# A second buffer for x in a 33-step attention loop: x fetched and normalized one step further ahead, its fold split around the fold of the weights, and the even half of the output copied into the output buffer

## What is computed

```python
q = fft(layernorm(x))              # along the 512 positions, per channel; x is (8, 512, 2048)
corr = ifft(q * conj(fft(ctx)))    # real part
w, idx = top_k(corr, 12); w = softmax(w)
out = sum_i w_i * ctx[min(idx_i + pos, 511)]
x = x + out
x = x + ffn(layernorm(x))          # routed low-rank FFN: gate from top 16 of 64 experts, z = x A^T, out = z_gated B^T
```

## Time and profile before

| | us |
|---|---|
| median of 3 runs | 2494.78 (2491.77 to 2495.44) |
| profiled execution, whole | 2492.05 |
| its span | 2490.2 |
| first `ctx_cyclic` of step 2 to that of step 27 (25 steps) | 132.73 to 1323.34 |
| steps 27 to 30 (no statistics in them) | 1323.34 to 1502.80 |

### The profile page before, as it was taken

One profiled execution on the slowest core, in us unless ns is written; L12 is line 12 of the kernel. 1 busy time (PEld: TensorE's weight loads), 2 busy tenths in 40 slices (PEclk: granted clock), 3 DMA queues, 4 the chain that ended last, 5 costly groups with the idle time before them and its releaser, 6 DMA issues.

```text
span 2490.2 us, 29447 instructions
## 1 busy us (share of the span) xinstructions
PE 2305.9 (93%) x9728; PEld 1560.6 (63%) x9728; DVE 1772.1 (71%) x3937; ACT 946.5 (38%) x1744; POOL 1567.6 (63%) x1006
## 2 busy tenths in 40 slices
PE   3799999999999999999999998669999999999999
PEld 1455655655655555565555565448878878878877
DVE  2787888788888888788878878745555555656652
ACT  2354344344444434434434534323333333333330
POOL 4887887888787887888788885534334333334330
PEclk7899999999999999999999999789999999999999
DMA  5224223223222322322321312544444444444431
GB/s 192 93 77 139 72 73 131 85 72 123 94 72 96 120 72 85 131 73 72 135 82 55 103 62 101 191 144 162 152 161 161 150 160 164 150 160 166 151 129 51
DMA packets 111468, 290.13 MB, mean 117 GB/s; under 512 B 7168, under 2 KB 7296, under 8 KB 110208
## 3 DMA queue, kind: packets, MB, share of 16 engines
q1 hardware_dynamic: 111360, 288.81, 33.6%
HBM read 221.68 MB, written 67.11 MB: 116 GB/s over the span
## 4 chain that ended last, share of the span: by engine, by line
PE 46%; POOL 31%; DMA 10%; DVE 6%; ACT 5%; issue 2%; SPq 0%; POOLq 0%; DVEq 0%; ACTq 0%
DMA xf<-in_x_dram 8%; POOL r_f L1217 8%; PE z L492 5%; PE out L492 5%; PE evac L509 5%; PE out L494 5%; PE out L493 5%; PE z L494 5%; PE z L493 5%; PE pair L522 4%; ACT xf L1010 4%; POOL xf L1200 3%; POOL half_fold L1207 3%; POOL half_fold L1197 3%; POOL half_fold L1198 3%; POOL xf L1201 3%
## 5 line engine op out<-in xcount | busy, mean ns | idle before, releaser
L1252 POOL TENSOR_TENSOR rows<-rows,cin 128x1024 f32<-128x1024 f32 x48 | 116.8, 2434 | 398.0 <-DMA rows<-out_dram 291.2
L593 PE MATMUL pair<-r_f,back 128*128 128x512 f32 x768 | 334.9, 592 | 1.5 <-DVE prod L787 1.5
L1217 POOL TENSOR_TENSOR r_f<-prod 128x1024 f32<-128x1024 f32 x128 | 302.6, 2384 | 17.7 <-DVE prod L787 17.7
L593 PEld LDWEIGHTS pair<-r_f,back 128*128 128x128 f32 x768 | 145.8, 190 | 171.9 <-issue 168.4
L565 PE MATMUL lag<-lags,p_f 128*128 128x256 f32 x1024 | 234.3, 382 | 12.9 <-DVE e L808 12.9
L492 PE MATMUL pair<-w_hi,wts_hi 128*128 128x512 f32 x512 | 206.9, 404 | 33.1 <-DVE w_lo L881 23.7
L565 PEld LDWEIGHTS lag<-lags,p_f 128*128 128x128 f32 x1024 | 193.8, 192 | 40.2 <-issue 13.8
L492 PE MATMUL out<-b_hi,zt_hi 128*128 128x512 f32 x512 | 208.0, 406 | 1.5 <-ACT zt_hi L1163 1.5
L492 PE MATMUL z<-a_hi,xt 128*128 128x512 f32 x512 | 207.6, 406 | 0.0
L1178 ACT ACTIVATE xt<-tp 128x512 fp32r<-128x512 f32 x128 | 73.1, 597 | 338.0 <-PE tp L637 338.0
L494 PE MATMUL z<-a_hi,xt 128*128 128x512 f32 x512 | 201.4, 393 | 0.0
(11 more groups left out here) (143 smaller groups left out, 5494.7 us busy)
## 6 DMA issues: line engine op xcount, KB each, us to landing
vf<-in_ctx_dram SPq DMA_DIRECT2D x32, 1024.0 KB, 5.1
xf<-in_x_dram SPq DMA_DIRECT2D x32, 1024.0 KB, 8.2
out_dram<-att_sb SPq DMA_DIRECT2D x32, 1024.0 KB, 5.2
rows<-out_dram SPq DMA_DIRECT2D x64, 512.0 KB, 3.7
cin<-out_dram SPq DMA_DIRECT2D x64, 512.0 KB, 4.1
xin<-in_x_dram SPq DMA_DIRECT2D x64, 512.0 KB, 3.7
out_dram<-rows SPq DMA_DIRECT2D x64, 512.0 KB, 2.6
stat_in<-in_x_dram SPq DMA_DIRECT2D x28, 1024.0 KB, 7.5
```

Of the source, the lines that this page charges most:

```text
L593: return nc.tensor.matmul(pair_ps[:, bank, :], back[:, 3 * bank + n, :], r_f[:, row, :], start=n == 0, stop=n == 2)
L1217: nc.gpsimd.tensor_tensor(dst, prod[:, slot, 0:2, :], prod[:, slot, 2:4, :], ALU.add).then_inc(add_done, 1)
L1252: nc.gpsimd.tensor_tensor(half, first, second, op).then_inc(c_added, 1)
```

## The change

Group g of x now lives in `xfs[g % 2]` with a semaphore `x_loaded[g % 2]` for each. SP loads group i+2 in step i, as its first DMA of the step, when PE has read group i; group 1 is loaded before the loop. The load of `stat_in` moves to after `v_last` and is made one step earlier. ACT normalizes group i+2 in step i, after the copies of the correlation and after `root`. POOL's `fold_x` is cut in two: `begin_fold_x(i+1)` stands between `fold_w` of tiles 0, 1 and of tiles 2, 3, and `end_fold_x(i+1)` stands after the products of x. `invert` on DVE and `normalizers` on POOL move from after the fourth product of the weights to after the second. ACT copies the even half of the output into `att_sb[:, 2:4]` instead of `even_sb`, and now waits for the store of the step before; DVE works in place on it. `first_tiles` no longer waits for products before it fetches `cin` and `xin`.

```diff
-        xf, vf, half_fold, stat_in = sb("xf", [P, 4, CH]), sb("vf", [P, 4, CH]), sb("half_fold", [P, 4, CH]), sb("stat_in", [P, LT, CH])
+        xfs = [sb(f"xf{n}", [P, 4, CH]) for n in range(2)]
+        vf, half_fold, stat_in = sb("vf", [P, 4, CH]), sb("half_fold", [P, 4, CH]), sb("stat_in", [P, LT, CH])
...
-                sp.dma_start(xf[:], at_group(x_t, k, r, off)).then_inc(x_loaded, 16)
+                sp.dma_start(xfs[(3 + r + off) % 2][:], at_group(x_t, k, r, off)).then_inc(x_loaded[(3 + r + off) % 2], 16)
...
+            load_x(-1, 1, 1)
...
-                if s and not is_step(i, 0):
-                    next_stat()
-                if f:
-                    sp.wait_ge(pair_ready, pair_x(i, 1) + 1)
-                    load_x(k, r, 1)
+                if i + 2 < GROUPS:
+                    sp.wait_ge(pair_ready, pair_x(i, 1) + 1)
+                    load_x(k, r, 2)
...
                     load_last(k, r, 1)
+                if (i - 2) // GPB + 2 < B:
+                    sp.wait_ge(stat_used, LT * (i + 3))
+                    load_stat((i - 2) // GPB, (i - 2) % GPB, stat_in[:], stat_loaded)
...
-                sp.wait_ge(prod_ready, prod_w(i, 3) + 1)
-                sp.wait_ge(dc_put, i)
                 for h in range(2):
                     load_others(0, 0, h)
...
-                if s and r == 3:
-                    invert(k + 2)
+                        if n == 1 and s and r == 3:
+                            invert(k + 2)
...
-                    if not is_step(i, 1):
-                        dve.wait_ge(stored, 16 * (i - 1))
-                    nc.vector.tensor_tensor(att_sb[:, 0:2, :], even_sb[:], pair_ps[:, 2:4, :], ALU.add)
-                    nc.vector.tensor_tensor(att_sb[:, 2:4, :], even_sb[:], pair_ps[:, 2:4, :], ALU.subtract).then_inc(att_done, 1)
+                    nc.vector.tensor_tensor(att_sb[:, 0:2, :], att_sb[:, 2:4, :], pair_ps[:, 2:4, :], ALU.add)
+                    nc.vector.tensor_tensor(att_sb[:, 2:4, :], att_sb[:, 2:4, :], pair_ps[:, 2:4, :], ALU.subtract).then_inc(att_done, 1)
...
-                if f:
-                    norm_inputs(k, r, 1)
-                    norm(k, r, 1, range(LT))
-                if a:
+                    if is_step(i, 0):
+                        norm_inputs(k, r, 1)
+                        norm(k, r, 1, range(LT))
                     minus(v_neg[cur][:, 5, :], v_neg[cur][:, 3, :], 6 * i + 6)
...
                 if s and r == 3:
                     root(k + 2)
+                if i + 2 < GROUPS:
+                    norm_inputs(k, r, 2)
+                    norm(k, r, 2, range(LT))
...
-                        act.wait_ge(att_done, i - 1)
-                    nc.scalar.activation(even_sb[:], pair_ps[:, 0:2, :], ACT.Copy).then_inc(even_copied, 1)
+                        act.wait_ge(stored, 16 * (i - 1))
+                    nc.scalar.activation(att_sb[:, 2:4, :], pair_ps[:, 0:2, :], ACT.Copy).then_inc(even_copied, 1)
...
-                    for t in range(CT):
+                    for t in (0, 1):
+                        fold_w(i - 1, t)
+                if f and b:
+                    begin_fold_x(i + 1)
+                if b:
+                    for t in (2, 3):
                         fold_w(i - 1, t)
...
                 if f:
-                    fold_x(i + 1)
+                    end_fold_x(i + 1)
                     begin_fold_v(i + 1)
...
+                        if n == 1 and s and r == 3:
+                            pool.wait_ge(normed, LT * (i + 2))
+                            normalizers(k + 2)
```

More of the change, by code:

```diff
@@ L165, in build_program @@
         r_f, back = sb("r_f", [P, 8, CH]), sb("back", [P, 12, P])
-        even_sb, att_sb = sb("even_sb", [P, 2, CH]), sb("att_sb", [P, 4, CH])
+        att_sb = sb("att_sb", [P, 4, CH])
         ones, rstd, shift = sb("ones", [P, 2]), sb("rstd", [P, LT]), sb("shift", [P, LT])
@@ L198, in build_program @@
         consts_set = sem("consts_set")
-        x_loaded, v_loaded, last_loaded, normed = sem("x_loaded"), sem("v_loaded"), sem("last_loaded"), sem("normed")
+        x_loaded = [sem(f"x_loaded{n}") for n in range(2)]
+        v_loaded, last_loaded, normed = sem("v_loaded"), sem("last_loaded"), sem("normed")
         x_half, x_ready, v_half, v_ready = sem("x_half"), sem("x_ready"), sem("v_half"), sem("v_ready")
@@ L376, in _ @@
             sp.dma_start(back[:].rearrange("p n m -> p (n m)"), tables["back"]).then_inc(tables_loaded, 16)
+            load_x(-1, 1, 1)
             def body(k, r, a, b, f, s):
                 i = 4 * k + 3 + r
-                def next_stat():
-                    sp.wait_ge(stat_used, LT * (i + 2))
-                    load_stat(k, r, stat_in[:], stat_loaded)
-                if s and not is_step(i, 0):
-                    next_stat()
-                if f:
-                    sp.wait_ge(pair_ready, pair_x(i, 1) + 1)
-                    load_x(k, r, 1)
-                if s and is_step(i, 0):
-                    next_stat()
+                if i + 2 < GROUPS:
+                    sp.wait_ge(pair_ready, pair_x(i, 1) + 1)
+                    load_x(k, r, 2)
+                if is_step(i, 0):
+                    sp.wait_ge(stat_used, LT * 2)
+                    load_stat(k, r, stat_in[:], stat_loaded)
                 if f:
@@ L521, in x_spectrum @@
                     for part, (t, fold) in enumerate(((4, 0), (1, 3)) if n == 0 else ((2, 2), (3, 1))):
-                        last = nc.tensor.matmul(pair_ps[:, 2 * n + part, :], fwd[:, t, :], xf[:, fold, :], start=True, stop=True)
+                        last = nc.tensor.matmul(pair_ps[:, 2 * n + part, :], fwd[:, t, :], xfs[i % 2][:, fold, :], start=True, stop=True)
                     last.then_inc(pair_ready, 1)
@@ L1009, in norm @@
                     t = slice(j, j + 1)
-                    nc.scalar.activation(xf[:, j, :], xf[:, j, :], ACT.Identity, bias=shift[:, t], scale=rstd[:, t]).then_inc(normed, 1)
+                    part = xfs[(3 + r + off) % 2][:, j, :]
+                    nc.scalar.activation(part, part, ACT.Identity, bias=shift[:, t], scale=rstd[:, t]).then_inc(normed, 1)
             def norm_inputs(k, r, off):
-                act.wait_ge(x_loaded, 16 * (4 * k + 3 + r + off) + 16)
+                g = 4 * k + 3 + r + off
+                act.wait_ge(x_loaded[g % 2], 16 * (g // 2 + 1))
                 act.wait_ge(norm_ready, NORM_OPS * (k + quarter(r, off)[1]) + NORM_OPS)
@@ L1190, in _, with begin_fold_x, end_fold_x @@
         def _(pool):
-            def fold_x(g):
+            def begin_fold_x(g):
+                xf = xfs[g % 2]
                 pool.wait_ge(normed, LT * g + LT)
-                if is_step(g, 1):
+                if g == 1:
                     pool.wait_ge(x_ready, 1)
                 else:
-                    pool.wait_ge(v_ready, max(g, 1) if isinstance(g, int) else g)
+                    pool.wait_ge(v_ready, max(g, 1))
                 nc.gpsimd.tensor_tensor(half_fold[:, 0:2, :], xf[:, 0:4:2, :], xf[:, 1:4:2, :], ALU.add)
                 nc.gpsimd.tensor_tensor(half_fold[:, 2:4, :], xf[:, 0:4:2, :], xf[:, 1:4:2, :], ALU.subtract).then_inc(x_half, 1)
+            def end_fold_x(g):
+                xf = xfs[g % 2]
                 pool.wait_ge(x_half, g + 1)
@@ L1262, in _ @@
             normalizers(0)
-            fold_x(0)
+            begin_fold_x(0)
+            end_fold_x(0)
             def body(k, r, a, b, f, s):
@@ L1276, in body @@
                         add_products(prod_x(i, n), n, p_f[:, 2 * n:2 * n + 2, :])
+                if is_step(i, 0):
+                    begin_fold_x(1)
                 if f:
-                    fold_x(i + 1)
+                    end_fold_x(i + 1)
                     begin_fold_v(i + 1)
@@ L1285, in body @@
                         add_products(prod_w(i, n), n % 2, r_f[:, 2 * blk:2 * blk + 2, :])
+                        if n == 1 and s and r == 3:
+                            pool.wait_ge(normed, LT * (i + 2))
+                            normalizers(k + 2)
                 if is_step(i, GROUPS):
                     add_x(1, 0, 1)
-                if s and r == 3:
-                    pool.wait_ge(normed, LT * (i + 2))
-                    normalizers(k + 2)
                 if f:
```

## The result

The changed kernel takes 2410.31 us (median of 4 runs, 2406.42 to 2414.86) against 2495.11 (4 runs), a ratio of 0.9663, 95% interval 0.9640 to 0.9686: 3.4% faster. The forecast was 2405 with a range of 2393 to 2430. The profiled execution took 2407.21 us, its span 2405.4, where before it was 2490.2.

The account below looks back on a forecast made before the run. The loop through x's load, norm and POOL's vf held PE, itself nearly full and the next bound. Savings of 85.3 us (steps 2 to 26) and 3.1 (27 to 30) took 2492.05 to 2403.7; named 2405, range 2393 to 2430.

Parts of the forecast that it names:

- What bounds the kernel before: Loop of 47.62 us a step: x's DMA, ACT's norm, then POOL until vf, for which PE waits; PE nearly full.
- A step of PE: 44.1: PE's step when nobody is late: step 15's 47.02 us less three stalls, 2.9 together, leaves 44.1.
- rival B: DVE's row update and POOL block each other: update up to 2.4 us later, 14.6 in all, 2420; chance 0.14.
- Load and norm ahead: x's transfer (7.84 us) and ACT's norm (2.94) leave the loop; the 1.4 us wait on w_lo goes.
- The split fold: begin_fold_x fits POOL's idle place before weigh; POOL ends 2.2 us early where it was 1.2 late.
- DVE: Product 2 no longer waits 4.07 us for POOL; output sum 0.6 into the next step; stalls on evac_sin go.
- Root steps: Seven steps with root: PE's spectrum 2 waits for DVE, 0.4 us per step; the moved norm costs nothing.
- Even half, SP, ends: Even-half copy and store, SP's load order, phase ends: no effect, the ends within 1 us either way.
- The sum: Steps 2 to 26 save 85.3 us, steps 27 to 30 save 3.1, the rest 0.
- A: DVE's chain, not PE, closes the new loop: steps of 44.9 us, 2427 on the median; chance 0.15.
- C: x's chain was not what held the step: it stays at 47, within 5 us of 2495; chance 0.03.
- D: Slower because the ctx transfer lands late among other DMA traffic: 2580 if it takes 18 us; chance 0.04.

Follow-up runs that it names:

- row_early: The changed kernel with DVE's one-row update moved from after the second evac_sin to right after the first; 2396.49 us.
- pool_plus1: row_early with one extra POOL sum of 128 x 512 in every step, just before end_fold_v; 2653.31 us in one run.
- no_split: The changed kernel with fold_x in one piece after the products of x, load and norm still a step ahead; 2430.23 us.
- norms_late: The changed kernel with DVE's invert and POOL's normalizers back after the fourth product of the weights; 2449.18 us.
- load_ahead: The changed kernel with ACT's norm and POOL's whole fold_x back at their old places, x still loaded a step ahead; 2433.23 us.
- row_short: The changed kernel with DVE's one-row update cut from 512 columns to 8, at its old place; 2404.30 us in one run.
- pool_plus3: row_early with three extra POOL sums of 128 x 512 in every step, just before end_fold_v; 2629.45 us in one run.
- pool_row_plus3: The changed kernel with the row update taken off DVE onto ACT and POOL, plus three extra POOL sums before end_fold_v in every step; 2488.91 us.

## Why the prediction was right, point by point

**What bounds the kernel before.** Right. With the load alone out of the loop the 47.2 became 44.9 and the DMA's share of the chain fell from 10 to 2%, while POOL kept 34%; with norm and fold moved as well POOL's fell to 2%, and the chain is PE's.

**A step of PE: 44.1.** The number came out (44.08), but by luck: two errors of 0.3 cancel. PE's own step is 43.8, seen in the four steps without statistics and in `row_early`. The 0.3 that I had too much: I took the idle time before a late matmul as the whole price of a stall, but the first matmul after it is slower as well. Step 15 of the kernel before, the two stalls of the earlier trace rows with their next instruction:

```profile
772.30 0.47 PE L492 MATMUL pair<-w_hi,wts_hi 128*128 128x512 f32 x1 [1.22 <-DVE w_lo L881]
772.61 0.40 PE L493 MATMUL pair<-w_lo,wts_hi 128*128 128x512 f32 x1
...
778.17 0.50 PE L492 MATMUL pair<-w_hi,wts_hi 128*128 128x512 f32 x1
778.50 0.40 PE L493 MATMUL pair<-w_lo,wts_hi 128*128 128x512 f32 x1
```

0.31 and 0.33 to the next start instead of 0.23, 0.2 for the two. Another 0.1 is in `ctx_cyclic`, 3.59 to the x matmuls instead of 3.69, where the first matmul after the stall of 1.67 takes 0.53 instead of 0.43. The other 0.3 that I had too little is the row update, rival B. I had DVE due 0.1 ahead of POOL; it is due 0.15 behind (769.91 against 769.76), so it loses. I priced this at 0.5 a plain step and 0.8 a root step, 14.6 in all; `row_early` gives back 0.28 and 0.45, 10.6 in the profiled 25 steps (2.6 of it the double loss of step 3) and 13.8 by the medians. So the mechanism to which I gave 0.14 came, and the time still fell into the range of the main forecast. The Trainium skill's rule in "SBUF — State Buffer", "Who interferes with whom", holds in kind: a DVE instruction with two SBUF inputs waited for a whole POOL instruction. In the changed kernel the wait is one instruction long, 2.1 us beside a sum of 2.38; in `pool_plus1` it went on through three ends, which is more than the rule says.

**Load and norm ahead.** Right: x lands and is normalized long before its use, `w_lo` is on time. The load is worth 62 us; the norm without the split adds 3, within the noise, since in one piece the fold holds up product 2.

**The split fold.** Right in its mechanism, and sized by `no_split` at 20 us, the lock's part in it not taken apart. POOL hands `vf` over at 797.54 and PE takes it at 799.23, 1.7 early where I had 2.2.

**DVE.** The output sum starts 0.9 into the step, where I had 0.6; product 2 waits for PE and not for POOL. Right, but for the row update.

**Root steps.** 44.72 instead of 44.5. The 0.4 that I kept for the aggregates is 0.45 by `row_early` (44.26 against 43.80), the rest is the lock. That `normalizers` had to move with the norm was named as the reason why it costs nothing, and `norms_late` shows the price of not moving them: 4.0 us in each step after a root step.

**Even half, SP, ends.** No effect, as said; the ends took about 1 us.

**The sum.** 88.4 forecast, 84.8 measured in the span. Steps 2 to 26 gave 81.5 instead of 85.3, of which 2.3 is step 3, whose double loss I had not thought possible, and 1.5 the root steps; steps 27 to 30 gave 4.3 instead of 3.1. Rivals A, C and D did not come: A's 44.9 is what `load_ahead` gives, without the two other parts.

## What to carry to other kernels

When a loop's chain runs through a transfer into a single buffer, put the load, its preparation and its place in the next engine's queue a step ahead together: the load alone left a quarter of the gain behind. Count a step's floor from start times of matmuls, and remember that a stall also slows the first matmul behind it. Before an engine's idle time is filled, look which short instruction of another engine has lived in it: here a row update of 0.67 us on DVE, harmless while POOL waited, grew to 2.8 once POOL ran without a pause, and to 8.6 with 1.3 us more of POOL work.

## What the runs showed of the hardware

The wait for the shared port is not bounded by one POOL instruction. The one-row update on DVE waited 2.1 us in most steps, 4.4 in step 3, and 7.8 to 8.3 in each of steps 2 to 30 of `pool_plus1` and in 17 of these 29 of `pool_plus3`, through three ends of POOL instructions at which it could have been let in. Even 1 x 8 elements waited 2.1 of 2.26. What decides who gets the port at such an end is open in part: in the changed kernel DVE won between the two sums of `end_fold_x`, in `pool_plus1` it lost there and won before `begin_fold_v`. One thing is the same in all 52 steps in which it lost at one end or more (steps 2 to 30; 6 in the changed kernel, `row_short`, `no_split` and `norms_late` together, 29 in `pool_plus1`, 17 in `pool_plus3`): each end at which it lost is one where the next POOL record begins before the last has ended, and it got in at the first where they leave a gap, 0.08 to 0.56 us and 0.14 in most (785.33 + 2.35 = 787.68 to 787.82 above). Such a gap is not needed: in most steps of the changed kernel it won where there is none.

PE's granted clock fell to its lower level for a short time in about half of the steps of `pool_row_plus3`, in which PE idles about 2 us at each start, and in the steps of `pool_plus1` with 6.5 us of idle time. The kernel before had it once in steps 2 to 30, although show 1.00 as the rounded mean: in step 24, just after PE's one stall of 2.0 us there, and that step, with 48.46 us, is the longest without `root`; with its other stalls, up to 1.7 us, it kept the upper level. The changed kernel kept it in step 3 through a stall of 2.0 too. The fall cost 1.5 us where two neighbouring steps can be compared.
